# Fused decoder layer: the gate's first chunks, the norm's second half and the bias fold in another order

## The reference

```
h = shift_token(x)                       # half of the channels come from the token before
q, k, v = split(h @ wqkv)                # 8 heads of 64, norms and rotary applied to q and k
x = x + local_attention(q, k, v) @ wo    # windows of 64
h = shift_token(x)
mu, var = h.mean(-1), h.var(-1)
h = (h - mu) / sqrt(var + 1e-05) * lg + lb
a, g = split(h @ w1 + b1)                # 341 each
x = x + (a * gelu(g)) @ w2 + b2
```

## Time and profile before

| | |
|---|---|
| median of 3 runs | 1802.85 us (1800.70 to 1802.86) |
| profiled execution | 1803.43 us |
| its span, first to last instruction | 1801.6 us |
| mean granted TensorE clock | 0.983 |
| busy share of the span | PE 94%, ACT 79%, DVE 57%, POOL 25% |
| instructions | 66568 |

### The profile page before, as it was taken

How to read it: one execution, slowest core, us unless ns; L and a number is a source line. 1 busy time by engine, 2 the same in 40 slices (tenths; PEclk the granted TensorE clock), 3 DMA queues, 4 the chain that set the end, 5 groups by cost and what they waited for, 6 DMA issues and landing times. The chain is left out here.

```text
span 1801.6 us, 66568 instructions
## 1 busy us (share of the span) xinstructions
PE 1695.7 (94%) x28128; PEld 1023.0 (57%) x28128; DVE 1019.7 (57%) x3178; ACT 1417.3 (79%) x2645; POOL 454.5 (25%) x387
## 2 busy tenths in 40 slices
PE   6998899999999999999999978999998889999988
PEld 4785555555555555555555435666663356666633
DVE  4566533333443333344432069999974489999844
ACT  4343799999999999999999947889872368888832
POOL 1115000000000000000000046777720277777300
PEclk9999899999999999999999989999999999999999
DMA  2000311111111111111100031111110001111100
GB/s 63 1 0 25 123 50 49 59 55 45 63 64 49 50 61 53 45 63 64 49 30 32 3 112 28 30 30 35 29 28 12 0 20 33 35 26 29 34 15 35
DMA packets 47419, 73.29 MB, mean 41 GB/s; under 512 B 8400, under 2 KB 38224, under 8 KB 47184
## 3 DMA queue, kind: packets, MB, share of 16 engines
q1 hardware_dynamic: 47184, 69.85, 12.6%
HBM read 21.08 MB, written 2.10 MB: 13 GB/s over the span
## 5 line engine op out<-in xcount | busy, mean ns | idle before, releaser
L690 ACT ACTIVATE x_probs<-x_pss 128x1024 f32<-128x1024 f32 x832 | 806.2, 1021 | 38.1 <-PE x_pss L611 6.9
L625 PE MATMUL x_acc<-x_probs,x_v 128*32 128x256 f32 x6656 | 436.9, 380 | 0.0
L611 PE MATMUL x_pss<-x_qx,x_kx 32*128 32x256 bf16 x9984 | 348.4, 270 | 6.7 <-ACT x_probs L690 1.9
L611 PEld LDWEIGHTS x_pss<-x_qx,x_kx 32*128 32x128 bf16 x9984 | 222.4, 93 | 190.7 <-ACT x_probs L690 171.6
L625 PEld LDWEIGHTS x_acc<-x_probs,x_v 128*32 128x32 f32 x6656 | 208.2, 110 | 83.3 <-issue 6.0
L737 DVE COPY x_vnext<-x_psp 128x128 f32<-128x128 f32 (+1 forms) x197 | 58.1, 295 | 314.3 <-PE x_psp L589 313.8
L1508 ACT ACTIVATE l_prob<-l_neg_sim,l_neg_top 128x128 f32<-128x128 f32 x512 | 198.1, 395 | 5.9 <-DVE l_neg_top L1330 5.9
L954 POOL TENSOR_TENSOR l_turned_half<-l_raw,l_tabB 128x512 f32<-128x512 f32 x128 | 186.9, 1481 | 47.8 <-ACT l_raw L1467 45.5
L666 POOL COPY x_zq<-zT 128x256 f32<-128x256 f32 x15 | 6.0, 401 | 749.3 <-PE x_psp L596 680.8
L1330 DVE CUSTOM_DVE_ANT_0 l_neg_sim<-l_pss,w_window,l_inv_norm 128x128 f32<-128x128 f32 x512 | 149.0, 348 | 5.1 <-issue 4.4
L964 POOL TENSOR_TENSOR l_direct<-l_direct,l_turned_half 128x1024 f32<-128x1024 f32 x64 | 150.9, 2357 | 0.0
(11 more groups left out here) (204 smaller groups left out, 2622.7 us busy)
## 6 DMA issues: line engine op xcount, KB each, us to landing
x_kx<-x_kp SPq DMA_DIRECT2D x96, 208.0 KB, 2.4
x_cT<-in_context SPq DMA_DIRECT2D x16, 832.0 KB, 4.6
x_qx<-x_qp SPq DMA_DIRECT2D x48, 192.0 KB, 2.3
l_vmid<-l_vt SPq DMA_DIRECT2D x64, 128.0 KB, 2.3
xT<-in_x SPq DMA_DIRECT2D x8, 256.0 KB, 5.4
shifted<-zT SPq DMA_DIRECT2D x32, 64.0 KB, 2.0
hs<-zT SPq DMA_DIRECT2D x32, 64.0 KB, 2.0
out_x<-xT SPq DMA_DIRECT2D x8, 256.0 KB, 2.0
```

The source lines that it names most:

```text
L611: ins = pe.matmul(pss[bank(k, 2 * p + r // 2)][:, r % 2, e, :], kx[par][rows, g, j * P:(j + 1) * P], qx[par][rows, g, a * S:(a + 1) * S], ...
L625: ins = pe.matmul(acc[32 * r:32 * r + 32, 0:S], v[:, j, g, r, :], probs[SLOT[p]][r // 2][:, r % 2, e, :], start=(u == 0), stop=(u == UNITS ...
L690: act.activation(probs[SLOT[p]][y][:, :, :, :], pss[bank(k, 2 * p + y)][:, :, :, :], ACT.Sigmoid, scale=HD ** -0.5).then_inc(weighed, 1)
```

## The change

In words:

- ScalarE loads Gelu's table right after `guess(0)`, does the remaining squares and chunk 0's three Gelus (the square of chunk 7 stands behind the first), then loads the logarithm's table again, makes `guess(1)`, and loads Gelu's table once more. The Gelu loop has chunks 1 to 7.
- VectorE scales chunks 0 to 3 and goes on to the gate. `center(7)` stands behind chunk 0's first gated tile and `refine(1)` behind its last; `scale(4)` and `scale(5)` behind chunk 2's first gated tile, `scale(6)` and `scale(7)` behind chunk 3's second.
- TensorE's four second-half spreads are split: two in chunk 2 between `widen(2,0)` and `widen(2,1)`, with `narrow(1)` moved behind `widen(2,1)`; two in chunk 3 behind `widen(3,1)`. They go to pss[1] and psq in turn and wait for the additions that free psq. `widen(3,2)` waits for all eight scalings.
- The chunks are written out on TensorE and VectorE, no longer in a loop.
- `fold` stands in turn -2 behind `project_k(0,0)` and uses pso; `make_bias` stands in VectorE's turn -2. The first batch's value product waits for it.
- At the attention's end the last transposition of the probabilities (`turn_over(LAST, 1, 1)`) stands before the value products and the fifth mean, and ScalarE's copies of them before the squares.

```
         def chunks(eng, body):
-            body(0, 0)
-            with eng.Fori(0, NCH // 2 - 1) as i:
-                for u in range(2):
-                    body(2 * i + 1 + u, 1 - u)
-            body(NCH - 1, 1)
+            for n in range(NCH):
+                body(n, n % 2)
...
@@ TensorE: turn, spread_out, chunk, end of the attention
                 project_k(later(x, 2), 0)
+                if isinstance(x[0], int) and x[0] == -2:
+                    fold()
                 project_v(x, 1)
...
-                elif c < 2:
+                elif c == 0:
                     pe.wait_ge(refined, (run * NG + g) * 2 + 2)
-                    pe.wait_ge(centered, base + NCH)
-                else:
-                    pe.wait_ge(scaled_out, base + n - 1)
+                    pe.wait_ge(gate_added, runs + 1)
+                elif c == 2:
+                    pe.wait_ge(scaled_out, base + 6)
+                    pe.wait_ge(gate_added, runs + 3)
...
             def chunk(n, u):
-                if isinstance(n, int) and n == 0:
-                    widen(0, 0)
+                widen(n, 0)
+                if n == 0:
                     mean_of(NCH - 1)
-                    widen(0, 1)
+                if n == 2:
+                    spread_out(1, 0)
+                    spread_out(1, 1)
+                elif n > 0:
+                    narrow(n - 1, 1 - u)
+                widen(n, 1)
+                if n == 0:
                     variances(1)
-                    widen(0, 2)
-                    for c in range(4):
-                        spread_out(1, c)
-                else:
-                    if isinstance(n, int) and n == 1:
-                        pe.wait_ge(scaled_out, base + NCH)
-                    widen(n, 0)
-                    narrow(n - 1, 1 - u)
-                    widen(n, 1)
-                    widen(n, 2)
+                if n == 2:
+                    pe.wait_ge(scaled_out, base + 6)
+                    narrow(1, 1)
+                if n == 3:
+                    spread_out(1, 2)
+                    spread_out(1, 3)
+                    pe.wait_ge(scaled_out, base + NCH)
+                widen(n, 2)
...
             score(LAST, 0)
-            fold()
             project_v(LAST, 1)
...
             mean_of(3)
+            turn_over(LAST, 1, 1)
             value(LAST, 0)
             mean_of(4)
-            turn_over(LAST, 1, 1)
             value(LAST, 1)
...
@@ VectorE: chunk, end of the attention
-                    if c == 0 and (not isinstance(n, int) or n > 0):
-                        add_gated(n - 1)
+                    if c == 0:
+                        if n == 0:
+                            center(NCH - 1)
+                        elif n == 2:
+                            scale(4)
+                            scale(5)
+                        else:
+                            add_gated(n - 1)
+                    if c == 1 and n == 2:
+                        add_gated(1)
+                    if c == 1 and n == 3:
+                        scale(6)
+                        scale(7)
+                if n == 0:
+                    refine(1)
...
             center(6)
-            scale(0)
-            center(7)
-            scale(1)
-            scale(2)
-            scale(3)
-            refine(1)
-            for n in range(4, NCH):
+            for n in range(4):
                 scale(n)
             chunks(dve, chunk)
...
@@ ScalarE: end of the attention and gate
             guess(0)
-            square_of(5)
-            square_of(6)
+            act.preload_act_table_set("gelu_and_others")
+            for n in range(4, 7):
+                square_of(n)
+            gate(0, 0)
             square_of(7)
+            gate(0, 1)
+            gate(0, 2)
+            act.preload_act_table_set("natural_log_exp_and_others")
             guess(1)
             act.preload_act_table_set("gelu_and_others")
-            with act.Fori(0, NCH) as n:
+            with act.Fori(0, NCH - 1) as i:
                 for c in range(HC):
-                    act.wait_ge(up, passes + HC * n + c + 1)
-                    act.activation(gelu[c], psg[c], ACT.Gelu,
-                                   bias=bias[:, HC + c:HC + c + 1]).then_inc(gelu_ready, 1)
+                    gate(i + 1, c)
```

More of the change, by code:

```diff
@@ L849, in local_and_gate @@
         var = [flat(pss[0]), flat(pss[1])]
-        wide = [[flat(pst[0]), flat(pst[1]), flat(pso), flat(psk)], [flat(psq), flat(pss[1]), flat(psq), flat(pss[1])]]
+        wide = [[flat(pst[0]), flat(pst[1]), flat(pso), flat(psk)], [flat(pss[1]), flat(psq), flat(pss[1]), flat(psq)]]
         psg, psa, psy = [flat(pss[0]), flat(pst[0]), flat(pso)], [psvy[:, :], flat(pst[1]), flat(psk)], flat(psq)
@@ L1097, in value @@
                     at_least(pe, o_ready, 2 * n + b)
+                    if isinstance(n, int) and n == 0 and b == 0:
+                        pe.wait_ge(bias_ready, layer + 1)
                     for h in range(2):
@@ L1155, in mean_of @@
                 elif n == 1:
-                    pe.wait_ge(bias_ready, layer + 1)
+                    pe.wait_ge(placed_q, 2 * B)
                 else:
@@ L1161, in fold @@
             def fold():
-                pe.wait_ge(placed_q, 2 * B)
                 for m in range(2 * HC):
-                    ins = pe.matmul(flat(psq)[:, m:m + 1], w["w1"][:, m * P:(m + 1) * P], w["ln_b"][:, 0:1], start=True, stop=True)
+                    ins = pe.matmul(flat(pso)[:, m:m + 1], w["w1"][:, m * P:(m + 1) * P], w["ln_b"][:, 0:1], start=True, stop=True)
                 ins.then_inc(folded, 1)
@@ L1198, in narrow @@
                 pe.wait_ge(gate_ready, passes + HC * (n + 1))
-                if isinstance(n, int) and n == 0:
-                    pe.wait_ge(scaled_out, base + NCH)
+                if n == 0:
+                    pe.wait_ge(centered, base + NCH)
                 else:
@@ L1207, in chunk @@
             def chunk(n, u):
-                if isinstance(n, int) and n == 0:
-                    widen(0, 0)
+                widen(n, 0)
+                if n == 0:
                     mean_of(NCH - 1)
-                    widen(0, 1)
-                    variances(1)
-                    widen(0, 2)
-                    for c in range(4):
-                        spread_out(1, c)
-                else:
-                    if isinstance(n, int) and n == 1:
-                        pe.wait_ge(scaled_out, base + NCH)
-                    widen(n, 0)
-                    narrow(n - 1, 1 - u)
-                    widen(n, 1)
-                    widen(n, 2)
+                if n == 2:
[5 more added lines that the diff above has]
+                if n == 0:
+                    variances(1)
+                if n == 2:
[6 more added lines that the diff above has]
+                widen(n, 2)
             assert HC == 3
@@ L1356, in turn @@
                 multiply_k(later(x, 2), 0)
+                if isinstance(x[0], int) and x[0] == -2:
+                    make_bias()
                 copy_v(x, 1)
@@ L1391, in make_bias @@
                 dve.wait_ge(folded, layer + 1)
-                dve.tensor_tensor(bias[:, :], flat(psq)[:, 0:2 * HC], w["b1"][:, :], ALU.add).then_inc(bias_ready, 1)
+                dve.tensor_tensor(bias[:, :], flat(pso)[:, 0:2 * HC], w["b1"][:, :], ALU.add).then_inc(bias_ready, 1)
             def center(n):
@@ L1425, in _ @@
             norm(LAST, 0, 0)
-            make_bias()
             center(0)
@@ L1541, in _, with gate @@
             act.preload_act_table_set("natural_log_exp_and_others")
+            def gate(n, c):
+                act.wait_ge(up, passes + HC * n + c + 1)
+                act.activation(gelu[c], psg[c], ACT.Gelu, bias=bias[:, HC + c:HC + c + 1]).then_inc(gelu_ready, 1)
             def square_of(n):
@@ L1567, in _ @@
             exps(LAST, 1, 1)
-            square_of(1)
             copy(LAST, 0, 1)
             copy(LAST, 1, 0)
+            square_of(1)
+            copy(LAST, 1, 1)
             square_of(2)
             copy_out(LAST, 0)
-            copy(LAST, 1, 1)
             square_of(3)
             copy_out(LAST, 1)
-            square_of(4)
             guess(0)
-            square_of(5)
-            square_of(6)
+            act.preload_act_table_set("gelu_and_others")
+            for n in range(4, 7):
+                square_of(n)
+            gate(0, 0)
             square_of(7)
+            gate(0, 1)
+            gate(0, 2)
+            act.preload_act_table_set("natural_log_exp_and_others")
             guess(1)
             act.preload_act_table_set("gelu_and_others")
-            with act.Fori(0, NCH) as n:
+            with act.Fori(0, NCH - 1) as i:
                 for c in range(HC):
-                    act.wait_ge(up, passes + HC * n + c + 1)
-                    act.activation(gelu[c], psg[c], ACT.Gelu,
-                                   bias=bias[:, HC + c:HC + c + 1]).then_inc(gelu_ready, 1)
+                    gate(i + 1, c)
```

## The result

The kernel after takes 1787.6 us (median of 9 runs, 1783.2 to 1795.0) against 1802.86 for the kernel before in the same rounds: ratio 0.992, 95% interval 0.9906 to 0.9933. A second comparison gave 1787.55 against 1805.1: 0.9898, interval 0.9881 to 0.9914. The forecast was 1786.8 us, range 1781 to 1794. That it came within 0.8 us is partly luck: the two comparisons put the gain at 15.3 and 17.6 us.

A forecast was written before the change was run, and what follows sets the result against it. TensorE bounds from chunk 1 on; before it, order starves TensorE. Savings 7.1 + 7.0 + 2 x 1.55 - 0.45 - 0.7 = 16.05 us from 1803.43 give 1787.4, less 0.58 for the median: 1786.8 us, range 1781 to 1794.

The forecast's parts named there:

- First spread to chunk 4: Norm's end and first chunks: 37.55 us, 7.1 less in layer 1 and 7.0 less in layer 0.
- ScalarE's detour: After chunk 0's gates: load, guess 1, load, 4.6 us in all, hidden by 0.8 to 0.9 us of slack before widen(2,0).
- slower rival: Detour stops TensorE before widen(2,0); decides from 8.8 us extra; at 10 us longer the kernel takes 1805.2 us; chance 0.03.
- The rule weighed: On ScalarE's table switches: finish one table set before switching; 2.66 us a load would make the sum about 4 us smaller.
- Clock at chunk 3's stop: Rival: granted clock falls at the stop before widen(3,2), costing 1.8 us a layer, 1790.4 us in all; chance 0.13.
- The fold out of the attention's end: Fold's 12 passes leave the attention's end, ending VectorE's waits on TensorE: 1.0 us less a layer, bounds 0 and 1.11.
- The last turn-over moved ahead: Attention's end, turn-over ahead of the value products: about 0.55 us less stall a layer, bounds 0 and 0.88.
- The fold in the first turn: Before project_q(0,1), delaying the keys GpSimd needs: 0.45 us more in layer 1, 0.7 more in layer 0.
- Loops written out: Chunks on TensorE and VectorE: bounded by 0.06 either way for four more chunks a layer, taken as nothing.

The follow-up runs named there:

- extra_loads: Kernel after with four more table loads on ScalarE behind guess(1): first spread to chunk 4 took 48.25 and 48.01 us.
- one_pair: Kernel after with two more table loads on ScalarE behind guess(1): first spread to chunk 4 took 41.31 us in both layers.
- gate_only: Kernel after with fold, bias addition and the attention's end in their old places, keeping the gate's early start: 1790.49 us against 1800.94 before, ratio 0.995.
- before_warm: Kernel before with two useless TensorE products ahead of the second half's first spread and two behind its last: 1803.69 us in one run.
- best: Kernel after with the wait for all eight scalings before narrow(3), variances(1) behind widen(0,2), fold later in the first turn: 1783.12 us, ratio 0.9878 to before.
- after again: The kernel after, unchanged, run and profiled a second time: 1787.55 us against 1805.1 for the kernel before.

## Why the prediction was right, and where its terms were off

- **First spread to chunk 4: forecast 37.55 us, measured 37.85.** The mechanism is right: the two stops stand where they were forecast, nothing stops TensorE before `widen(2,0)`, and the clock is 1.00 throughout chunks 0 to 2. The stops were smaller than priced, 0.25 and 1.82 instead of 2.4 in all, and the first later pair of spreads took 1.06 (1723.71 to 1724.77) instead of 1.13. What was left out is the change from one kind of product to another: behind the variances a product takes 0.96 us (1712.24 to 1713.20), the next one 0.86. There are seven such changes in the stretch; at 0.1 each, an estimate, they make some 0.7 us, which the sum had priced at nothing. No run took them one by one.
- **ScalarE's detour: forecast 4.6 us with 0.8 to 0.9 of slack, measured 4.62 and 0.84.** The slower rival was far from its point of decision: 8.8 us of extra detour at full clock. extra_loads shows that the price past the slack was set too low, since a long stop brings half clock with it: 5.12 us of loads cost 10.2 to 10.4 a layer, and 2.56 in one_pair cost 3.46. Between the two (an estimate) some 4 us of extra detour, not 8.8, would have eaten a layer's gain of 7.4.
- **The rule weighed.** The Trainium skill, ScalarE: Activation LUTs, "What ACT_TABLE_LOAD costs", puts a drain of some 1.38 us on top of each load. No run here shows it: behind each of the seven loads in the two ScalarE views above, the next load or activation starts within 0.02 us. The two sets were switched twice more a layer, and it paid.
- **Clock at chunk 3's stop: forecast as a rival, 0.13, at 1.8 us a layer.** It happened in two of ten layers, at 1.58. It is not a state of the kernel but of a layer in a run, so the forecast should have had a part of it in the sum: 0.2 x 1.58 x 2 = 0.6 us.
- **The fold out of the attention's end: forecast -1.0, measured -0.86.** The size is near, the account is not quite that of the prediction, which counted VectorE's waits for TensorE, 1.11 in all. TensorE was the bound there: it lost 1.36 us of work (1694.54 to 1695.90), and in place of VectorE's waits one of its own for VectorE appeared, 0.41 at 1686.82, which the prediction had not looked for.
- **The last turn-over moved ahead: forecast -0.55, measured -0.17.** This is the step whose mechanism was wrong. The 0.88 us of the earlier trace rows was ScalarE's wait, on an engine that was not the bound there. TensorE had only a short wait for that copy, 0.21 by the weight load at 1711.30 above, so most of the 0.88 had nothing to give back; its marks there, from the fourth mean to the variances, are 4.84 us apart before and 4.67 after.
- **The fold in the first turn: forecast +0.45 and +0.7.** The delay is there where it was looked for: GpSimd's second half starts 0.32 us later in layer 1 (5.47 to 5.79 behind the layer's start) and 0.53 in layer 0 (6.94 to 7.47), with 0.4 to 0.7 forecast, and in best, with the later fold, layer 1 is back at 5.47. What the stage pays is not settled. Layer 1 took 264.76 to 264.97 us in six profiles with the early fold and 265.44 in a seventh, but 264.32, 263.87 and 266.18 in the three without a fold in that turn (before, gate_only, before_warm). Layer 0 took 267.06 to 267.97 with it, and 267.13, 268.75 and 267.92 without. So the measured +0.51 and +0.65 of layer 1 fit the forecast, and the 0.84 and 0.19 of layer 0 surround it, but the same stage differs by up to 2.3 us between kernels in which it is the same.
- **Loops written out: forecast 0, within 0.06 a chunk.** Layer 0 0.00; layer 1 -0.21 to -0.23, 0.07 a chunk (7.91 to 7.84), just past the bound. No run has the loops alone, and why layer 1's were slower is not shown.

The forecast's 1.05 us too much in the attention's end and 0.6 too much in the norm's end were partly made up by layer 0's fold (0.5 cheaper than forecast) and layer 1's loops (0.2); layer 1's fold was 0.2 dearer. That is how 16.05 became the 14.94 of the pair before and after again; the parts in the first turn are smaller than what that stage differs without an edit, so there the agreement is luck as much as insight.

## What to carry to other kernels

Price a stop on TensorE twice, by its length and by what the clock does behind it: the stop of 1.82 us was free of the second in eight of ten layers, that of 4.20 was doubled in both. Read the idle time of the engine that sets the pace, not of the one that is easiest to see waiting. A total that agrees with a theory proves little; look for the row in which the mechanism would have to stand.

## What the runs showed of the hardware that was not expected

- The same stop of 1.82 us, behind the same work, was followed by half clock in two of ten layers; with a stop of 1.62 us some 18 us before it (one_pair), in two of two, though the first of the two stops left the clock at 1.00.
- After the stop of 4.20 us the clock stayed at 0.50 for 8 us of unbroken work, and 4.2 us were lost in that chunk alone.
- From a layer's start to its last score, kernels with the same code there differ by up to 2.3 us, and nearly all of it arises before the seventh of some 30 scores: from there on, the twelve profiles agree within 0.2 us.
- One kernel's layer 0 started at 1051.86 us in one execution and at 1057.45 in another: 5.6 us of difference in work of a millisecond, more than any single term here but the norm's end. A difference of two totals, each from one run, can't tell such terms.
